# A four-layer graph network on one core: one-hots read from PSUM and moved to ScalarE, node rows gathered by tile, stores moved to the next stage, a statistics instruction in the layer norms

## The reference

```
x = _layernorm(x + _L0_gnn_ref(x, ...))   # mean over (source, relation) of the destination rows, relation weights, relu
x = _layernorm(x + _L1_gnn_ref(x, ...))   # deg = 1 + segment_sum(1, dst); h = x @ W; sums of h[src] per dst; batch norm
x = _layernorm(x + _L2_gnn_ref(x, ...))   # attention over edges (4 heads of 128), own layer norm, feed forward
x = _layernorm(x + _L3_gnn_ref(x, ...))   # two transformer convolutions (4 heads of 32)
_layernorm(x): m = mean(x); v = var(x); (x - m) / sqrt(v + 1e-5)
```

## Time and profile before

| what | value |
|---|---|
| median of three runs | 4256.2 us (4242.35 to 4259.15) |
| profiled execution, its own time | 4245.88 us |
| its span | 4244.1 us |
| granted TensorE clock, mean | 0.821 |
| PE busy / DVE busy / POOL busy / ACT busy | 3122.9 / 2654.0 / 2499.5 / 801.6 us |

### The profile page before, as it was taken

One profiled execution on the slowest core, in us unless ns is written; L12 is line 12 of the kernel. 1 busy time (PEld: TensorE's weight loads), 2 busy tenths in 40 slices (PEclk: granted clock), 3 DMA queues, 4 the chain that ended last, 5 costly groups with the idle time before them and its releaser, 6 DMA issues. The chain is left out here.

```text
span 4244.1 us, 59998 instructions
## 1 busy us (share of the span) xinstructions
PE 3122.9 (74%) x14813; PEld 1957.0 (46%) x14814; DVE 2654.0 (63%) x8500; ACT 801.6 (19%) x2009; POOL 2499.5 (59%) x2771
## 2 busy tenths in 40 slices
PE   6988976636666635999997899965676876667773
PEld 3445865424444421444443344453354663345652
DVE  8986754351111249788887888884375774365875
ACT  3840000010000003000000677650010110010111
POOL 0027777737777605766663788703777751777760
PEclk8985556768888857999998999987887987889886
DMA  1111222221111112666662222203687863677871
GB/s 63 51 49 45 56 56 56 54 47 51 51 51 51 42 31 64 173 166 166 164 169 72 62 69 67 60 7 106 182 237 193 257 199 87 182 215 216 254 227 48
DMA packets 383723, 466.66 MB, mean 110 GB/s; under 512 B 56179, under 2 KB 284944, under 8 KB 383482
## 3 DMA queue, kind: packets, MB, share of 16 engines
q0 software_dynamic: 84864, 219.09, 20.9%
q1 hardware_dynamic: 298618, 244.58, 19.0%
HBM read 349.37 MB, written 114.10 MB: 109 GB/s over the span
## 5 line engine op out<-in xcount | busy, mean ns | idle before, releaser
L1844 POOL DMA_INDIRECT got<-kv_table,pair_src x832 | 824.7, 991 | 552.9 <-issue 368.1
L603 POOL DMA_INDIRECT y_got<-y_table,y_idx x416 | 450.0, 1082 | 404.7 <-POOLq L57 278.2
L1009 POOL DMA_INDIRECT got<-t_table,pair_src x416 | 412.6, 992 | 192.8 <-issue 126.2
L2055 PE MATMUL psum<-acc 125*128 x1664 | 288.0, 327 | 204.5 <-DVE h L1907 180.2
L1203 PE MATMUL sums<-msg,hot 128*125 128x512 f32 x832 | 404.5, 635 | 29.4 <-POOL msg L1144 29.4
L2067 PE MATMUL psum<-h,acc 128*128 128x128 f32 x1664 | 331.2, 335 | 77.2 <-ACT hot_b L2031 53.1
L1431 POOL DMA_INDIRECT got<-x_table,pair_src x312 | 294.3, 943 | 154.9 <-issue 152.0
L2055 PEld LDWEIGHTS psum<-acc 125*128 125x128 f32 x1664 | 248.2, 227 | 280.6 <-issue 279.5
L1019 DVE TENSOR_TENSOR hot<-pair_dst,iota 128x500 f32<-128x500 f32 x112 | 76.0, 684 | 457.2 <-PE gcn_psum L1085 456.8
L1470 DVE SCALAR_TENSOR_TENSOR small<-z,att 128x128 f32<-128x128 f32 x1248 | 287.0, 286 | 94.0 <-PE z L1535 94.0
L1907 DVE TENSOR_TENSOR h<-psum,got 128x512 f32<-128x512 f32 x208 | 143.1, 688 | 316.6 <-DMA got<-kv_table,pair_src 284.7
(11 more groups left out here) (490 smaller groups left out, 5724.5 us busy)
## 6 DMA issues: line engine op xcount, KB each, us to landing
v_rows<-got SPq DMA_DIRECT2D x208, 256.0 KB, 3.8
small<-v_rows SPq DMA_DIRECT2D x208, 256.0 KB
dst_row<-dst_rows SPq DMA_DIRECT2D x312, 125.0 KB
rows<-x_rows SPq DMA_DIRECT2D x104, 256.0 KB, 2.6
x_rows<-got SPq DMA_DIRECT2D x104, 192.0 KB, 2.1
got<-kv_table,pair_src POOLq DMA_INDIRECT x832, 4.1
y_table<-y_stage SPq DMA_DIRECT2D x25, 500.0 KB
y_got<-y_table,y_idx POOLq DMA_INDIRECT x416, 2.6
```

Of the source, the lines that this page charges most:

```text
L603: pool.indirect_dma_start(out=got[:, slot, j, :], out_offset=None, in_=y_table[:, :], in_offset=bass.IndirectOffsetOnAxis(ap=m.y_idx[:, co ...
L1009: pool.indirect_dma_start(out=self.got[:, slot, j, :], out_offset=None, in_=self.table[:, :], in_offset=bass.IndirectOffsetOnAxis(ap=self. ...
L1844: pool.indirect_dma_start(out=got[:, slot, j, :], out_offset=None, in_=kv_table[:, :], in_offset=bass.IndirectOffsetOnAxis(ap=m.pair_src[: ...
L2055: last = t.matmul(work[:, j * P:(j + 1) * P], hot_t[:, g % 2, j // 2, j % 2, :], m.acc[:, bass.ds(ws[j], 1), 0:D].rearrange("q o d -> q (o ...
```

## The change

Six edits. (1) In the count loop and in `gcn_sums` the one-hots compare with a copy of the iota that lies in PSUM. (2) The degrees' lane one-hot `dl` is made by ScalarE: `Abs(iota - loc)` for each of four tiles, then `Relu(1 - that)` over the group; TensorE waits for a semaphore more. (3) `gcn_sums` gathers per tile (392) and not per pair (416), into a ring of 12 groups, 48 slots; TensorE reads a second small table, `slot_i`, for the slot of each pair. A slot is used by pairs up to six groups (`ROOM`) behind its gather. (4) The store of `m.x` into `x_table` moves to the beginning of `gat_nodes`, that into `wide_table` is cut into 25 pieces ahead of each `left` store. (5) `layer_norm` takes mean and variance from one `bn_stats` per window and applies both with one two-scalar instruction per window. (6) `conv_nodes` goes through the windows twice, 256 columns each time, k and v first. `SL` becomes 33.

```diff
-YS, Y_EARLY, SL, RB = 6, 6, 34, 104
+YS, Y_EARLY, SL, RB = 6, 6, 33, 104
+NS, ROOM = 12, (W - 1) // 4
 def layer_norm(...):
-    link(v.reduce_sum(mean, x, AX))
-    link(v.tensor_scalar(mean, mean, 1.0 / D, None, ALU.mult))
-    link(v.tensor_tensor(y, x, bc_last(mean, D), ALU.subtract))
     for w in range(W):
-        last = v.scalar_tensor_tensor(tmp[:, w, :], y[:, w, :], 1.0, y[:, w, :], ALU.mult, ALU.mult, accum_out=var[:, w:w + 1])
+        last = v.bn_stats(six[:, w, :], x[:, w, :])
     link(last)
+    link(v.tensor_tensor(var, six[:, :, 2], six[:, :, 5], ALU.add))
+    link(v.tensor_tensor(mean, even, odd, ALU.add))
+    link(v.tensor_tensor(even, even, odd, ALU.subtract))
+    link(v.scalar_tensor_tensor(odd, even, 0.25 * D, even, ALU.mult, ALU.mult))
+    link(v.tensor_tensor(var, var, odd, ALU.add))
     v.tensor_scalar(var, var, 1.0 / D, eps, ALU.mult, ALU.add).then_inc(var_ready, 1)
+    link(v.tensor_scalar(mean, mean, 0.5, None, ALU.mult))
     dve.wait_ge(std_ready, turn)
-    link(v.reciprocal(mean, var))
-    link(v.tensor_tensor(y, y, bc_last(mean, D), ALU.mult))
+    link(v.reciprocal(var, var))
+    for w in range(W):
+        last = v.tensor_scalar(y[:, w, :], x[:, w, :], mean[:, w:w + 1], var[:, w:w + 1], ALU.subtract, ALU.mult)
+    link(last)
...
 def relation_layer(...):
+            link(v.tensor_copy(ps[2][:, 0:P], m.iota[:, 0:P]))
-                v.tensor_tensor(hot_c[:, g % 4, :, :], bc_last(src_loc[:, g * G:(g + 1) * G], P), bc_mid(m.iota[:, 0:P], G),
+                v.tensor_tensor(hot_c[:, g % 4, :, :], bc_last(src_loc[:, g * G:(g + 1) * G], P), bc_mid(ps[2][:, 0:P], G),
                                 ALU.is_equal).then_inc(hots, 1)
...
-                    v.tensor_tensor(dl[:, b, :, :], bc_last(dst_loc[:, at], P), bc_mid(m.iota[:, 0:P], G), ALU.is_equal)
                     v.tensor_tensor(dw[:, b, :, :], ...).then_inc(deg_hots, 1)
...
+            act.wait_ge(loc_ready, 1)
+            for g in range(TILES // G + 1):
+                if g < TILES // G:
+                    if g >= 2:
+                        act.wait_ge(dl_ready, g - 1)
+                    for j in range(G):
+                        last = s.activation(away[:, g % 2, j, :], m.iota[:, 0:P], ACT.Abs, bias=dst_loc[:, g * G + j:g * G + j + 1])
+                    last.then_inc(away_ready, 1)
+                if g:
+                    act.wait_ge(away_ready, g)
+                    if g >= 3:
+                        act.wait_ge(used, g - 2)
+                    s.activation(dl[:, (g - 1) % 2, :, :]..., away[:, (g - 1) % 2, :, :]..., ACT.Relu, scale=-1.0, bias=ones[:, 0:1]
+                                 ).then_inc(dl_ready, 1)
...
 def gcn_sums(...):
-            loop.gathers(pool, lambda g, slot: pool.wait_ge(used, g + 1))
+            for g in range(tile_groups):
+                if g >= NS:
+                    pool.wait_ge(used, g - NS + ROOM + 1)
+                for j in range(G):
+                    col = g * G + j
+                    pool.indirect_dma_start(out=got[:, col % ring, :], ..., ap=m.tile_src[:, col:col + 1] ...).then_inc(come[g % NS], 16)
...
+            for g in range(groups):
+                ws = windows(nc, m.pair_win_i, ENG.PE, g * G, G)
+                at = windows(nc, slot_i, ENG.PE, g * G, G, ring - 1)
+                pe.wait_ge(hot_ready, g + 1)
+                if g < tile_groups:
+                    pe.wait_ge(come[g % NS], 16 * G * (g // NS + 1))
+                for j in range(G):
+                    last = t.matmul(sums[0:Q, bass.ds(ws[j] * D, D)], hot[:, g % 8, j, :], got[:, bass.ds(at[j], 1), :]..., ...)
+                last.then_inc(used, 1)
+                if g < tile_groups - ROOM:
                     keep_busy(t, sums[0:Q, 6 * 512:7 * 512], zeros, Q, 6)
...
 def batch_norm(...):
-            sp.dma_start(nodes(x_table)[:, :, 0:D], m.x[:, :, :]).then_inc(stored, 16)
-            sp.dma_start(nodes(wide_table)[:, :, 0:D], m.x[:, :, :]).then_inc(stored, 16)
-            sp.wait_ge(stored, 32)
 def gat_nodes(...):
+            sp.dma_start(nodes(x_table)[:, :, 0:D], m.x[:, :, :]).then_inc(stored, 16)
             sp.wait_ge(lin_ready, 1)
...
             for w in range(W):
+                sp.dma_start(wide_table[w * Q:(w + 1) * Q, 0:D], m.x[:, w, :]).then_inc(stored, 16)
                 sp.wait_ge(left_kept, w + 1)
...
 def conv_nodes(...):
-            for w in range(W):
+            for n in range(2 * W):
+                half, w = divmod(n, W)
...
-                nc.tensor.matmul(ob[w % 4][0:Q, :], xt[:, w, :], w4[:, :, :]..., start=True, stop=True).then_inc(done, 1)
+                nc.tensor.matmul(ob[n % 4][0:Q, 0:2 * D], xt[:, w, :], w4[:, 2 * half:2 * half + 2, :]..., start=True, stop=True).then_inc(done, 1)
```

More of the change, by code:

```diff
@@ L978, with windows @@
 WG = 2 * G
-def windows(nc, wins, engine, at, n):
+def windows(nc, wins, engine, at, n, top=W - 1):
     cols = slice(at, at + n) if isinstance(at, int) else bass.ds(at, n)
     _, values = nc.values_load_multi_w_load_instructions(
-        wins[0:1, cols], engines=[engine], min_val=0, max_val=W - 1, skip_runtime_bounds_check_because="a pair's window is a count of 24 comparisons")
+        wins[0:1, cols], engines=[engine], min_val=0, max_val=top, skip_runtime_bounds_check_because="a pair's window is a count of 24 comparisons")
     return values
@@ L1033, in gcn_sums @@
         sb, sem, bank = scope(nc, ctx)
-        loop = PairLoop(nc, m, ctx, table, hots=8)
+        ring, come, groups, tile_groups = NS * G, m.come_tile, PAIRS // G, TILES // G
+        got, hot = sb("got", [P, NS * G, D]), sb("hot", [P, 8, G, Q])
+        slot_i, slot_f, turn_f = sb("slot_i", [1, PAIRS], I32), sb("slot_f", [1, PAIRS]), sb("turn_f", [1, PAIRS])
+        hot_ready, slots_ready = sem("hot_ready"), sem("slots_ready")
         zeros = sb("zeros", [P, 512], BF16)
-        sums = m.gcn_psum
+        sums, iota = m.gcn_psum, bank("iota_psum")
         used, zeroed, done = sem("used"), sem("zeroed"), sem("all_summed")
@@ L1058, in _, with one_hots @@
             nc.vector.memset(zeros[:, :], 0.0).then_inc(zeroed, 1)
-            for slot in range(loop.slots):
-                loop.one_hots(slot * G, slot)
+            v = nc.vector
             link = make_link(dve, chain)
+            def one_hots(g):
+                v.tensor_tensor(hot[:, g % 8, :, :], bc_last(m.pair_dst[:, g * G:(g + 1) * G], Q), bc_mid(iota[:, 0:Q], G),
+                                ALU.is_equal).then_inc(hot_ready, 1)
+            link(v.tensor_copy(iota[:, 0:Q], m.iota[:, 0:Q]))
+            link(v.tensor_tensor(slot_f[:, :], m.iota[0:1, 0:PAIRS], m.pair_win[0:1, :], ALU.subtract))
+            link(v.tensor_scalar(turn_f[:, :], slot_f[:, :], 1.0 / ring, 0.5 / ring - 0.5, ALU.mult, ALU.add))
+            link(v.tensor_scalar(turn_f[:, :], turn_f[:, :], ROUND, None, ALU.add))
+            link(v.tensor_scalar(turn_f[:, :], turn_f[:, :], ROUND, None, ALU.subtract))
+            link(v.scalar_tensor_tensor(slot_f[:, :], turn_f[:, :], -float(ring), slot_f[:, :], ALU.mult, ALU.add))
+            v.tensor_copy(slot_i[:, :], slot_f[:, :]).then_inc(slots_ready, 1)
+            for g in range(8):
+                one_hots(g)
             dve.wait_ge(loaded, 48)
@@ L1065, in _ @@
             link(nc.vector.tensor_tensor(m.x_beta[:, :, :], m.x[:, :, :], bc_mid(m.gcn_vec[0:Q, 2, :], W), ALU.add))
-            with dve.Fori(0, loop.steps) as i:
-                for slot in range(loop.slots):
-                    g, at = loop.slots * i + slot, i * (loop.slots * G) + slot * G
-                    dve.wait_ge(used, g + 1)
-                    loop.one_hots(at + loop.slots * G, slot)
+            for g in range(8, groups):
+                dve.wait_ge(used, g - 7)
+                one_hots(g)
             dve.wait_ge(done, 1)
@@ L1077, in _ @@
             clear_banks(t, zeros, sums, False)
-            with pe.Fori(0, loop.steps) as i:
-                for slot in range(loop.slots):
-                    g, at = loop.slots * i + slot, i * (loop.slots * G) + slot * G
-                    ws = windows(nc, m.pair_win_i, ENG.PE, at, G)
-                    pe.wait_ge(loop.hot_ready, g + 1)
-                    pe.wait_ge(loop.come[slot], 64 * i + 64)
-                    for j in range(G):
-                        last = t.matmul(sums[0:Q, bass.ds(ws[j] * D, D)], loop.hot[:, slot, j, :], loop.got[:, slot, j, :],
-                                        start=False, stop=False)
-                    last.then_inc(used, 1)
+            pe.wait_ge(slots_ready, 1)
+            for g in range(groups):
[5 more added lines that the diff above has]
+                for j in range(G):
+                    last = t.matmul(sums[0:Q, bass.ds(ws[j] * D, D)], hot[:, g % 8, j, :],
+                                    got[:, bass.ds(at[j], 1), :].rearrange("l o d -> l (o d)"), start=False, stop=False)
+                last.then_inc(used, 1)
+                if g < tile_groups - ROOM:
```

(6 more changed lines are left out.)

49 lines of the change are left out of this document (30 added, 19 removed).

## The result

The changed kernel takes 4113.88 us in the median of three runs (4112.11, 4113.88, 4120.03), the kernel before 4249.27 in the median of four (4240.55 to 4259.15). A fourth run of the changed kernel took 6942.18 us; it is a slow one and enters no comparison. The ratio is 0.9684, with a 95% interval of 0.9649 to 0.9719: 3.2% faster. The profiled execution took 4120.03 us. Its page begins with this line, which answers to the earlier trace rows.

What follows compares the result with a forecast made beforehand. Blocks run one behind another, each bound by what it waits for last, GpSimd's gathers in relation_layer and gcn_sums. Gains of 131 us from the profiled 4245.9 give 4115, some 4125 for the runs' median; forecast 4122 us, range 4095 to 4165.

Steps and rivals of the forecast that it cites:

- relation_layer, 47 us: In relation_layer, gathers no longer lengthened by VectorE one-hots: 21.2 us in the count loop, 29.2 less 3 in the second.
- the sum: Whole kernel: 47 + 31 + 34 + 15 + 5 - 1 = 131 us gained.
- So it is the second SBUF operand: Gathers lengthen beside VectorE instructions reading two SBUF tensors; the iota in PSUM takes that away; undisturbed 943 ns from gat_scores.
- the term for `dw`: Second loop of relation_layer: `dw` stays on VectorE and keeps lengthening gathers, taken as 3 us of the 29.2 us excess.
- ScalarE hidden: Second loop of relation_layer: ScalarE's new one-hots take about 2.2 us a group, hidden behind TensorE first and gathers later.
- The point of 3.85 us: Second loop of relation_layer: ScalarE's time a group beyond which the block's end moves later.
- gcn_sums, 31 us: In gcn_sums, 42 us from 24 fewer gathers and less lengthening, minus 11 us net given back at the end.
- The alternatives stated there for the tail: End of gcn_sums: net gain 24 us at 2.87 us a group, 34 at 1.68, instead of 31 at 2.0.
- The stores, 34 us: Moving stores: batch_norm loses 39 us, ScalarE's wait in gat_nodes grows by 5.2; net 34 us, bounds 20 and 39.
- Norm, 3 us each: Each layer norm falls from 17.0 to 14.1 us, so 3 us a norm and 15 in five.
- The wide bounds: Layer norm: bn_stats 0.15 to 0.35 us, two-scalar instruction 0.21 to 0.41; from 25 us gained to 19 lost.
- conv_nodes, 2.5 us each: In conv_nodes, the first store starts earlier: 2.5 us a block, 5 in two, bounds 0 and 8.

Runs made afterwards that it cites:

- The fp32 copies: Changed kernel with unused VectorE work added in gcn_sums: fp32 SBUF-to-SBUF copies, then two-operand sums, then bf16 copies, in one run; 4986.37 us.

## Why the prediction came out right

- **relation_layer, 47 us.** 50.3 by the block's length, which differs by some 10 us between executions of the same code; the 416 gathers took 49.5 us less. The count loop gave 22.8 by itself (21.2 in the sum) and the second loop 27.4 (26.2). Where this was argued from the gathers' duration, the runs show it: the two edits alone move 1395 ns to 945 and 1044 to 948, each only in its own loop.
- **"So it is the second SBUF operand".** Right for the instructions that the change touches, of 0.67 us and more, and not a rule. The fp32 copies show that a one-operand form lengthens gathers too. And the stage that the argument took its undisturbed 943 ns from also ran 412 instructions of 288 ns with two operands in SBUF, which lengthened nothing. The sum met this only in the term for `dw`: 3 us by "a shorter instruction blocks less", where the second loop's excess after the change is 287 x 0.007 = 2 us.
- **ScalarE hidden.** 2.0 us a group instead of 2.2; it waited 187 us for TensorE, and TensorE never for it. The point of 3.85 us was not measured, as told above.
- **gcn_sums, 31 us.** 35.8. The mis-sized term is the tail: a group with two table reads takes 1.4 us at the end, not 2.0, and from the last landing to the block's end it was 1384.6 - 1371.8 = 12.8 us instead of 17. The excess over undisturbed gathers fell from 412.6 - 392.7 = 20 us to 377.8 - 370.0 = 8, by 12 us, as in the sum. The alternatives stated there for the tail come out of its own terms as 25 and 33 us, not 24 and 34.
- **The stores, 34 us.** 33.8 alone. ScalarE's wait grew by 4.9 us, forecast 5.2.
- **Norm, 3 us each.** 3.5 in gcn_nodes by its instructions, and 15 in all five by the lengths of their blocks, as in the sum (with 2.3 of batch_norm's 41.7, of which the stores alone explain 39.4). The statistics follow each other at 4.93 / 25 = 0.20 us (I took 0.22), the two-scalar instructions at 6.49 / 25 = 0.26 (0.27). The wide bounds for these unseen prices were not needed. Their upper end was added up wrongly: 0.15 and 0.21 us an instruction would have gained 31 us, not 25.
- **conv_nodes, 2.5 us each.** 1.7 over many profiles, with the reserve told above, and in the profile of after 2.5 gained in one and 1.3 lost in the other. The sum's reason, an earlier first store, held only in the first: it was issued 11.2 us after the block's start (13.9 before), in the second 14.1 (12.9).
- **The sum.** 131 us against 135 between the medians, and 4122 us against 4113.88. Part of that agreement is luck: the changed blocks of the profiled execution lost 137, and the others grew by 11 that the parts can't explain. Most of this is one conv_layer of 610.4 us. The two conv_layers took 600.1 to 607.5 us in the four kernels with one part of the change, which leave them alone, so this one lies 2.9 us above that spread. The 1 us for extra instructions was not measured by itself.

## What to carry to other kernels

Where GpSimd's gathers bound a stage, look at what VectorE runs beside them before looking at the gathers. An fp32 instruction with two SBUF tensors cost them 0.16 to 0.43 us for each us of its own at 0.7 us length and 0.63 at 1.9 us, a fast fp32 copy 0.46. The same work with an operand in PSUM, as four short instructions with a number per lane, or on ScalarE cost next to nothing, and so did short instructions (under 0.3 us) of either form. A block that waits for its own stores can hand them to the next one, but then the order on the issuing queue is what to plan: 3125 small rows stopped it for some 8 us wherever they stood, so they belong where the consumers have buffers to spare. And read a part's worth from the length of its block, not from the call, and in a block with gathers see whether they come down to their undisturbed duration.

## What I had not expected of the hardware

- A gather beside two fp32 copies from SBUF to SBUF, one behind the other (128x1664 in 1.04 us each), took 2.16 us instead of 0.944, and one beside a sum of two operands 2.51. But 412 instructions of 0.288 us with two operands in SBUF left the gathers beside them at 0.943.
- The issue of a store that follows 3125 small rows takes 7.5 to 8.8 us on SyncE's queue, wherever in the changed gat_nodes it stands (5.7 in the kernel before).
- The same program took 4247 us on one chip and 5068 and 5127 on two others, with VectorE's instructions as long as before and holes of some 6 us, put down to "remote", in relation_layer's second loop; the other stages with gathers are longer too. Its cause is open.
